# Closing two key or value sums at once on the two halves of TensorE's array

## The chip, the cores and the metric

The kernel runs on one core of a Trainium2 chip, as one program in one launch. The metric is the device time of one execution in microseconds. It is compared as the median of several runs.

## The reference

A decoder of two layers is computed for 8 sequences of 112 tokens with 256 features. Each layer has an attention of its own kind, a cross-attention to a context, and a feed-forward part, each followed by a layer norm. The change lies in the cross-attention of the first layer:

```python
x = _layernorm(x + _L0_xattn_ref(x, ctx_768, Wq, Wk, Wv, Wo, bo), axis=-1)

def _L0_xattn_ref(x, context, Wq, Wk, Wv, Wo, bo):     # x (8,112,256), context (8,375,192)
    h, dh = (16, 64)
    q = (x @ Wq).reshape(B, Nq, h, dh)
    k = (context @ Wk).reshape(B, Nk, h, dh)            # Wk, Wv (192, 1024)
    v = (context @ Wv).reshape(B, Nk, h, dh)
    scores = jnp.einsum('bqhd,bkhd->bhqk', q, k) * dh ** -0.5
    attn = jax.nn.softmax(scores, axis=-1)
    out = jnp.einsum('bhqk,bkhd->bqhd', attn, v).reshape(B, Nq, h * dh)
    return out @ Wo + bo
```

The keys and values of all 8 sequences, `context @ Wk` and `context @ Wv`, are what the change touches. They contract over 192 features, which is one block of 128 and one of 64.

## The kernel before

**The products of keys and values.** TensorE computes them in the format fp32r (F32R in the code), in which one pass of an instruction handles a matmul that takes two passes in fp32. Since one fp32r product is rounded, each operand is split into a rounded high part and the remainder, the low part, and several products are added in one PSUM bank. The main block (128 features) takes three: high x high, high x low, low x high. The second block has 64 features; the host lays these out twice, in rows 0 to 63 and 64 to 127. `ctx_rest` holds the rounded high part of the context in the upper 64 rows and its low part in the lower 64, so that the fourth pass `rest x rest` gives high x high and low x high of that block at once. The fifth pass, `last`, multiplies `ctx_rest` by `w_rest_low`, the low part of the weights, in all 128 rows: high x low and low x low. `exact_products` (L96) lists the five pairs and `accumulate` (L82) issues them; its matmul is at L86. A sixth tensor, `rest_high`, has the rounded high part of the second block in all 128 rows. GpSimd makes it (L670, L794) for its own subtraction, and no matmul reads it.

**Sizes.** A key sum ("k" job) gives 128 of the 1024 key features for 375 context positions (376 columns in the matmul); 8 make the keys of a sequence. A value sum ("v" job) gives 512 value features for 125 positions; 6 make the values.

**Rounds and jobs.** `cross_attention` (from L683) works in rounds -1 to 8. In round i, TensorE computes the heads of sequence i, the queries, keys and values ("front") of sequence i + 1, and the end ("tail") of sequence i - 1. A round has 8 steps u. In each step, TensorE issues in this fixed order: the transposes of the probabilities (`turn`, L845), the scores of the next step (`scores`, L836), the weighing with the values of the step before (`weigh`, L857), and then two or three jobs. The jobs share PSUM banks 0 and 1. The front jobs come in pairs, one on bank 0 and the next on bank 1: u = 0 has q0 and q1, u = 1 to 4 the eight k, u = 5 to 7 the six v. Others come between: in rounds with a tail, job OUT (the output projection) goes ahead of the pair of u = 2 on bank 1, and job NT (transposes at L893) ahead of the pair of u = 5 on bank 1. RB follows the pair of u = 0 on bank 0. In rounds with heads, RA comes at u = 6 on bank 0, behind the pair if there is one: transposes of the softmax divisors at L886. Round -1 has neither heads nor tail, only the front jobs of sequence 0, one behind the other, with the first scores behind step 4.

**Who empties the banks.** Each job's last matmul adds one to `job_ready[b]`. ScalarE then copies bank 0 (L1021, queries L1022), VectorE copies bank 1 (L936, queries L937; OUT is read by L968), and each adds one to `job_used[b]`. A job begins with a wait on `job_used` of its bank for all earlier jobs there. TensorE executes its instructions in order, so a wait at the start of a job holds everything behind it. VectorE's order per step is: copy the turned probabilities (L949), maximum of the next scores (L944), empty bank 1. ScalarE's is: exponentials of the next scores (L1028), empty bank 0.

**Halves of the array.** In `scores`, the two heads of a step have 64 rows each, in rows 0 to 63 and 64 to 127, and write to different banks. In `weigh`, the two heads write to different halves of the output partitions, 64 columns of the array each. The wide cross-attention of the second layer has in its `scores` (L1241, L1244) two matmuls over 128 rows, followed by two over 64 rows each.

Of the kernel before, what the change touches and what calls it, by code (L numbers as in the profile page):

```python
# [19 lines left out]
ST, SP_ = 3, S // 3  # L20
SE = S + 1
CB = DC - 128
# [59 lines left out]
def accumulate(pe, out, pairs):  # L82

    last = None
    for k, (lhs, rhs) in enumerate(pairs):
        last = pe.matmul(out, lhs, rhs, start=(k == 0), stop=(k == len(pairs) - 1))  # L86
    return last
# [8 lines left out]
def exact_products(lhs, rhs):  # L96

    return [(lhs["high"], rhs["high"]), (lhs["high"], rhs["low"]), (lhs["low"], rhs["high"]),  # L100
            (lhs["rest"], rhs["rest"]), (lhs["last"], rhs["last"])]


def wait_past(eng, sem, value):

    if not isinstance(value, int) or value > 0:
        eng.wait_ge(sem, value)
# [22 lines left out]
class Core:  # L130
# [36 lines left out]
    def sem(self, name):  # L167
        self.phase_sems.append(self.nc.alloc_semaphore(name=name))
        return self.phase_sems[-1]
# [513 lines left out]
def cross_attention(core, d, layer):  # L683
# [8 lines left out]
    bank = core.bank  # L692
# [32 lines left out]
    def before(i, b):  # L725

        if isinstance(i, int):
            extra = max(i, 0) + max(i - 1, 0) if b == 0 else 2 * max(i - 1, 0)
            return U * min(i + 1, B) + extra
        return (U + 2) * i + (U - 1 if b == 0 else U - 2)  # L730

    with ExitStack() as ctx:
# [3 lines left out]
        ctx_t, ctx_high, ctx_low, ctx_rest, rest_high = core.ctx_t, core.ctx_high, core.ctx_low, core.ctx_rest, core.rest_high  # L736
        w_high, w_low, w_rest, w_rest_low = core.w_high, core.w_low, core.w_rest, core.w_rest_low
        kt, v, qt = pair("kt", [128, M, S]), pair("v", [SP_, ST, INNER]), pair("qt", [128, M, T])
# [9 lines left out]
        job_ready, job_used = [sem("job_ready0"), sem("job_ready1")], [sem("job_used0"), sem("job_used1")]  # L748
# [27 lines left out]
        with nc.Block() as block:  # L776
            @block.sync
            def _(sp):
                for i in range(2, B):
                    wait_past(sp, split_done, i - 3)  # L780
                    sp.dma_start(ctx_t[i % 2][:, :, :], d["ctx_t"][i].rearrange("(c p) n -> p c n", p=128)).then_inc(ctx_loaded[i % 2], 16)
# [40 lines left out]
            @block.tensor  # L822
            def _(pe):
                ident = core.c(128, C_ID, 128)
                context = lambda q, cols: dict(high=ctx_high[q][:, cols], low=ctx_low[q][:, cols], rest=ctx_rest[q][:, cols],
                                               last=ctx_rest[q][:, cols])
                weights = lambda n, cols: dict(high=w_high[n][:, cols], low=w_low[n][:, cols], rest=w_rest[n][:, cols],
                                               last=w_rest_low[n][:, cols])

                def scores(i, u, p):  # L830
                    if u == 0:
                        pe.wait_ge(job_used[0], before(i - 1, 0) + QK // 2 + (0 if isinstance(i, int) and i <= 1 else 1))
                        pe.wait_ge(job_used[1], before(i - 1, 1) + QK // 2 + (0 if isinstance(i, int) and i <= 1 else 1))
                    for e in range(PER):
                        rows = slice(e * DH, (e + 1) * DH)
                        last = pe.matmul(S_BANK(u, e)[0:T, 0:S], qt[p][rows, u, :], kt[p][rows, u, :], start=True, stop=True)  # L836
                    last.then_inc(s_ready, 1)

                def turn(i, u):
                    for e in range(PER):  # L840
                        pe.wait_ge(p_ready, (i * U + u) * PER + e + 1)
                        if e == 0:
                            wait_past(pe, pt_copied, (i * U + u) * PER)
                        for k in range(ST):
                            last = pe.transpose(T_BANK(u, e)[0:SP_, k * T:(k + 1) * T], PROB(u, e)[:, k * SP_:(k + 1) * SP_], ident[0:T, 0:T])  # L845
                        last.then_inc(pt_ready, 1)

                def weigh(i, u, p):
                    if u == U - 1:
                        pe.wait_ge(pt_copied, (i + 1) * G)  # L850
                    if u % HU == 0:
                        wait_past(pe, ot_ready, 2 * i - 1 + u // HU)
                    at = u % HU * T
                    for k in range(ST):
                        for e in range(PER):
                            g = u * PER + e
                            last = pe.matmul(bank[6 + u // HU][e * DH:(e + 1) * DH, at:at + T], v[p][:, k, g * DH:(g + 1) * DH],  # L857
                                             prob_t[u % 2][e][:, k, :], start=(k == 0), stop=(k == ST - 1))
                    last.then_inc(pv_done, 1)

                def job(i, p, b, n, kind, a):
                    q = 1 - p
                    heads, out = parts(i)[0], bank[b]
                    wait_past(pe, job_used[b], before(i, b) + n)
                    if kind == "q":
                        for m in range(4):
                            last = accumulate(pe, out[:, m * T:(m + 1) * T], [
                                (core.wq[:, c, (4 * a + m) * 128:(4 * a + m + 1) * 128], core.xt[:, c, bass.ts(i + 1, T)])
                                for c in range(KD)])
                    elif kind == "k":  # L870
                        if a == 0:
                            wait_past(pe, split_done, i)
                            if not heads:
                                pe.wait_ge(w_split, 1)
                        last = accumulate(pe, out[:, 0:SE], exact_products(
                            weights("k", slice(a * 128, (a + 1) * 128)), context(q, slice(0, SE))))
                    elif kind == "v":
                        if a == 0 and not heads:
                            pe.wait_ge(w_split, 2)
                        last = accumulate(pe, out[0:SP_, :], exact_products(  # L880
                            context(q, slice(a // 2 * SP_, (a // 2 + 1) * SP_)), weights("v", slice(a % 2 * 512, (a % 2 + 1) * 512))))
                    elif kind in (RA, RB):
                        pe.wait_ge(inv_ready, 2 * i + (1 if kind == RA else 0))
                        for m in range(HU):
                            u = a * HU + m
                            last = pe.transpose(out[:, m * T:(m + 1) * T], inv[:, u * 128:(u + 1) * 128], ident[0:T, 0:T])  # L886
                    elif kind == OUT:
                        pe.wait_ge(ot_ready, 2 * i)
                        last = accumulate(pe, out[0:T, 0:D], [(ot[:, m, :], core.wo[:, m, :]) for m in range(M)])
                    else:  # L890
                        pe.wait_ge(normed_ready, i)
                        for c in range(KD):
                            last = pe.transpose(out[:, c * T:(c + 1) * T], normed[:, c * 128:(c + 1) * 128], ident[0:T, 0:T])  # L893
                    last.then_inc(job_ready[b], 1)

                def round_(i, p):
                    heads, front, tail = parts(i)
                    for u in range(U):
                        if heads:
                            turn(i, u)  # L900
                            if u + 1 < U:
                                scores(i, u + 1, p)
                            elif front:
                                scores(i + 1, 0, 1 - p)
                            if u > 0:
                                weigh(i, u - 1, p)
                        if tail and u == 0:
                            weigh(i - 1, U - 1, 1 - p)
                        for b, n, kind, a in jobs(u, heads, front, tail):
                            job(i, p, b, n, kind, a)  # L910
                        if front and not heads and u == U_KEYS:
                            scores(i + 1, 0, 1 - p)

                rounds(pe, round_)
# [1422 lines left out]
```

## Time and profile before

| | us |
|---|---|
| median of 3 runs | 1117.83 (1116.03 to 1121.14) |
| the profiled execution | 1118.2 |
| its span, first to last instruction | 1116.4 |
| TensorE matmuls busy in the span | 1018.3 (91%) |
| TensorE weight loads busy | 784.8 (70%), beside the matmuls |
| VectorE, ScalarE, GpSimd busy | 579.7, 404.0, 151.0 |
| mean granted TensorE clock | 0.945 of 2.4 GHz |

The span is the time between the first and the last instruction in the trace of one execution; its whole time is 1.8 us more. Matmuls overlap in the trace: a record lasts longer than the step to the next record, so that the sum of durations is no time. The step from one start to the next is what one of a series costs. A matmul in fp32 leaves two records, one for each pass; one in fp32r leaves one. The first cross-attention lies between 126.9 and 476 us.

### The profile page before, as it was taken

How to read it: one execution, taken by the hardware profiler on the slowest of the kernel's cores; microseconds unless marked ns; L12 is line 12 of the kernel's file. 1: busy time of each engine (PE TensorE's matmuls, PEld its weight loads, DVE VectorE, ACT ScalarE, POOL GpSimd, SP SyncE). 2: the span in 40 equal slices, each digit the busy share in tenths (PEclk: the TensorE clock that was granted, in tenths of full speed). 3: DMA queues.
4: the chain of work that ended last, by engine and by line, in shares of the span. 5: the costliest groups of instructions: out<-in, count | busy, mean ns of one | idle time of the engine just before them, and what ended most of it. 6: DMA issues, size and time to landing. Idle time of an engine off the chain costs nothing. (4 is left out here: it accounts for less than half of the span.)

```text
span 1116.4 us, 17912 instructions
## 1 busy us (share of the span) xinstructions
PE 1018.3 (91%) x6672; PEld 784.8 (70%) x6672; DVE 579.7 (52%) x1271; ACT 404.0 (36%) x1029; POOL 151.0 (14%) x151
## 2 busy tenths in 40 slices
PE   6899799999999999779999978787899999999884
PEld 4578677787787776579999964455767777776642
DVE  1786545555555555565556553575244444444315
ACT  2556434333333334254444513466233222322100
POOL 0334311011011000023333412100100000000000
PEclk9999899999999999979999998899899999999955
DMA  4500000000000000092111003300000000010001
GB/s 143 183 2 1 29 14 11 6 14 15 0 0 0 0 0 0 1 312 66 50 38 38 1 1 66 67 2 1 28 1 21 9 14 14 15 27 1 1 0 33
DMA packets 24159, 34.21 MB, mean 31 GB/s; under 512 B 3153, under 2 KB 19762, under 8 KB 24098
## 3 DMA queue, kind: packets, MB, share of 16 engines
q1 hardware_dynamic: 24098, 33.39, 10.0%
q8 instruction: 39, 0.64, 0.2%
q14 instruction: 22, 0.18, 0.1%
HBM read 30.63 MB, written 2.75 MB: 30 GB/s over the span
## 5 line engine op out<-in xcount | busy, mean ns | idle before, releaser
L1028 ACT ACTIVATE x_prob<-bank,x_negmax 112x375 f32<-112x375 f32 x128 | 72.2, 569 | 154.0 <-DVE x_negmax L944 154.0
L1661 DVE TENSOR_TENSOR moe_h_low<-moe_sq,moe_h_high 128x448 fp32r<-128x448 f32 x64 | 54.7, 872 | 52.8 <-ACT moe_h_high L1726 39.6
L1702 POOL TENSOR_TENSOR moe_sq<-moe_r 128x448 f32<-128x448 f32 x64 | 64.0, 1002 | 123.2 <-ACT moe_r L1734 104.7
L86 PE MATMUL bank<-moe_w_low,moe_h_high 128*112 128x256 f32 x256 | 71.8, 280 | 0.0
L86 PE MATMUL bank<-moe_w_high,moe_h_high 128*112 128x256 f32 x256 | 71.7, 280 | 0.0
L86 PE MATMUL bank<-moe_w_high,moe_h_low 128*112 128x256 f32 x256 | 71.7, 280 | 0.0
L944 DVE TENSOR_REDUCE x_negmax<-bank 112x1 f32<-112x375 f32 x128 | 64.1, 542 | 8.0 <-PE bank L836 6.0
L1734 ACT ACTIVATE moe_r<-bank 128x448 f32<-128x448 f32 x64 | 34.9, 545 | 86.9 <-PE bank L86 85.3
L1427 ACT ACTIVATE x_prob<-bank,x_negmax 112x375 f32<-112x375 f32 x64 | 36.1, 568 | 72.6 <-DVE x_negmax L1342 72.6
L949 DVE COPY x_prob_t<-bank 125x336 f32<-125x336 f32 x128 | 58.9, 498 | 6.1 <-PE bank L845 4.2
L857 PEld LDWEIGHTS bank<-x_prob_t,x_v 125*64 125x64 f32 x768 | 37.7, 137 | 34.2 <-issue 30.2
L836 PE MATMUL bank<-x_kt,x_qt 64*112 64x375 f32 x256 | 57.1, 523 | 0.7 <-DVE x_kt L936 0.7
L845 PE MATMUL bank<-const,x_prob 112*125 112x112 f32 x384 | 54.1, 276 | 2.6 <-ACT x_prob L1028 2.4
L845 PEld LDWEIGHTS bank<-const,x_prob 112*125 112x125 f32 x384 | 50.9, 190 | 6.2 <-ACT x_prob L1028 4.8
L86 PE MATMUL bank<-w_in,xt 128*112 128x512 f32 (+2 forms) x128 | 44.6, 490 | 11.3 <-DMA w_in<-in_L_attn_W_in 8.5
L86 PE MATMUL bank<-moe_xt_high,moe_w_high 128*128 128x448 f32 x128 | 48.5, 379 | 3.9 <-DVE moe_w_low L1667 2.7
L857 PE MATMUL bank<-x_prob_t,x_v 125*64 125x112 f32 x768 | 51.4, 270 | 0.0
L1241 PE MATMUL bank<-x_ctx_t,x_qt 128*112 128x375 f32 x128 | 46.8, 488 | 3.5 <-ACT x_prob L1427 2.9
L810 POOL COPY x_inv<-x_inv_head 112x512 f32<-112x512 f32 x16 | 9.8, 614 | 282.3 <-DVE x_inv_head L955 282.3
L1342 DVE TENSOR_REDUCE x_negmax<-bank 112x1 f32<-112x375 f32 x64 | 32.0, 542 | 30.6 <-PE bank L1244 30.6
L86 PE MATMUL bank<-moe_xt_low,moe_w_high 128*128 128x448 f32 x128 | 47.6, 372 | 0.0
L86 PE MATMUL bank<-moe_xt_high,moe_w_low 128*128 128x448 f32 x128 | 47.5, 371 | 0.0
(365 smaller groups left out, 2290.3 us busy)
## 6 DMA issues: line engine op xcount, KB each, us to landing
moe_w<-in_L_ffn_W SPq DMA_DIRECT2D x16, 512.0 KB, 4.7
ctx_t<-in_ctx_t SPq DMA_DIRECT2D x8, 376.0 KB, 4.3
x_ctx_t<-in_ctx_t SPq DMA_DIRECT2D x8, 376.0 KB, 3.1
wk<-in_L_xattn_Wk SPq DMA_DIRECT2D x2, 1024.0 KB, 6.7
wv<-in_L_xattn_Wv SPq DMA_DIRECT2D x2, 1024.0 KB, 9.5
wq<-in_L_xattn_Wq SPq DMA_DIRECT2D x2, 1024.0 KB, 11.5
wo<-in_L_xattn_Wo SPq DMA_DIRECT2D x2, 1024.0 KB, 13.1
w_in<-in_L_attn_W_in SPq DMA_DIRECT2D x1, 1160.0 KB, 7.1
```

The lines of the kernel that those rows point to most:

```text
L86: last = pe.matmul(out, lhs, rhs, start=(k == 0), stop=(k == len(pairs) - 1))
L836: last = pe.matmul(S_BANK(u, e)[0:T, 0:S], qt[p][rows, u, :], kt[p][rows, u, :], start=True, stop=True)
L845: last = pe.transpose(T_BANK(u, e)[0:SP_, k * T:(k + 1) * T], PROB(u, e)[:, k * SP_:(k + 1) * SP_], ident[0:T, 0:T])
L857: last = pe.matmul(bank[6 + u // HU][e * DH:(e + 1) * DH, at:at + T], v[p][:, k, g * DH:(g + 1) * DH], prob_t[u % 2][e][:, k, :], start=(k ...
L944: dve.tensor_reduce(negmax[:, g:g + 1], S_BANK(u, e)[0:T, 0:S], AX_X, ALU.max, negate=True).then_inc(max_ready, 1)
L949: dve.tensor_copy(prob_t[u % 2][e][:, :, :], T_BANK(u, e)[0:SP_, 0:ST * T] .rearrange("s (k t) -> s k t", k=ST)).then_inc(pt_copied, 1)
L1028: act.activation(PROB(u, e)[:, :], S_BANK(u, e)[0:T, 0:S], ACT.Exp, bias=negmax[:, g:g + 1], accum_out=total[:, g:g + 1]).then_inc(p_ready, 1)
L1241: pe.matmul(S_BANK[e][0:T, 0:S], q[:, 2 * j + e, query], c[:, 0, 0:S], start=True, stop=False)
L1427: act.activation(prob[w % 2][e][:, :], S_BANK[e][0:T, 0:S], ACT.Exp, bias=negmax[:, g:g + 1], accum_out=total[:, g:g + 1]).then_inc(e_read ...
L1661: dve.tensor_tensor(h_low[half][:, m, :], sq[m % 2][:, :], h_high[half][:, m, :].bitcast(F32), ALU.subtract).then_inc(low_done, 1)
L1702: pool.tensor_tensor(sq[m % 2][:, :], r[m % 2][:, :], r[m % 2][:, :], ALU.mult).then_inc(sq_done, 1)
L1734: act.activation(r[m % 2][:, :], bank[m][:, 0:HALF], ACT.Relu).then_inc(h_used, 1)
```

## The change

The list of products has four pairs instead of five. A "k" or "v" job on bank 0 now issues its four passes without closing the sum and without announcing it. The job on bank 1 issues its own four, and then `close_sums` issues the fifth pass of both. Each of these is over 64 rows: the sum in bank 0 takes rows 0 to 63 of `w_rest_low` and `rest_high`, the sum in bank 1 takes rows 64 to 127, which hold the same features. It gives high x low of the second block; low x low is not computed any more. Both `job_ready` are announced by these two matmuls.

```diff
-    return [(lhs["high"], rhs["high"]), (lhs["high"], rhs["low"]), (lhs["low"], rhs["high"]),
-            (lhs["rest"], rhs["rest"]), (lhs["last"], rhs["last"])]
+    return [(lhs["high"], rhs["high"]), (lhs["high"], rhs["low"]), (lhs["low"], rhs["high"]), (lhs["rest"], rhs["rest"])]
...
+                def open_sum(out, pairs):
+
+                    for k, (lhs, rhs) in enumerate(pairs):
+                        pe.matmul(out, lhs, rhs, start=(k == 0), stop=False)
+
+                def close_sums(q, kind, a):
+
+                    for b in range(2):
+                        half, at = slice(b * CB, (b + 1) * CB), a + b
+                        if kind == "k":
+                            last = pe.matmul(bank[b][:, 0:SE], w_rest_low["k"][half, at * 128:(at + 1) * 128], rest_high[q][half, :],
+                                             start=False, stop=True)
+                        else:
+                            last = pe.matmul(bank[b][0:SP_, :], rest_high[q][half, at // 2 * SP_:(at // 2 + 1) * SP_],
+                                             w_rest_low["v"][half, at % 2 * 512:(at % 2 + 1) * 512], start=False, stop=True)
+                        last.then_inc(job_ready[b], 1)
...
-                        last = accumulate(pe, out[:, 0:SE], exact_products(
-                            weights("k", slice(a * 128, (a + 1) * 128)), context(q, slice(0, SE))))
+                        open_sum(out[:, 0:SE], exact_products(weights("k", slice(a * 128, (a + 1) * 128)), context(q, slice(0, SE))))
+                        if b == 1:
+                            close_sums(q, "k", a - 1)
+                        return
...
-                        last = accumulate(pe, out[0:SP_, :], exact_products(
+                        open_sum(out[0:SP_, :], exact_products(
                             context(q, slice(a // 2 * SP_, (a // 2 + 1) * SP_)), weights("v", slice(a % 2 * 512, (a % 2 + 1) * 512))))
+                        if b == 1:
+                            close_sums(q, "v", a - 1)
+                        return
```

## Rows read from the trace of the kernel before

**Rows 1.** Windows: length, busy us and count of each engine, clock, DMA share.

```profile
192.00:233.00 41.00, 40.96 (x304) 32.06 (x304) 22.87 (x52) 15.03 (x44) 4.29 (x8) 1.00 0.04 11
...
126.90:476.00 349.10, 337.37 (x2432) 262.88 (x2432) 193.40 (x420) 122.42 (x354) 34.39 (x47) 0.98 0.03 7
```

**Rows 2.** Waits, 126.9 to 476 us: waited for, us in total, times, longest.

```profile
PEld bank L86 <- DVE xt L936: 2.8, 6, 0.5
...
PE bank L86 <- DVE x_qt L937: 1.6, 1, 1.6
```

**Rows 3.** Timeline, end of the stage: start, us, what.

```profile
475.24 0.37 SPq L1537 DMA_DIRECT2D moe_wg<-in_L_ffn_Wg  x1
```

**Rows 4.** Groups by line and form, 126.9 to 476 us, TensorE.

```profile
L86 PE MATMUL bank<-ctx_rest,wk_rest_low 128*128 128x376 f32 x64 | 21.5, 335 | 0.0
...
L86 PE MATMUL bank<-wv_rest_low,ctx_rest 128*125 128x512 f32 x48 | 18.8, 392 | 0.0
```

**Rows 5.** Timeline, the end of two key sums and the next step.

```profile
249.99 0.33 PE L86 MATMUL bank<-ctx_high,wk_low 128*128 128x376 f32 x1
...
251.19 0.80 PEld L845 LDWEIGHTS bank<-const,x_prob 112*125 112x125 f32 x6
251.37 0.81 PE L845 MATMUL bank<-const,x_prob 112*125 112x112 f32 x6
...
252.10 0.89 PE L836 MATMUL bank<-x_kt,x_qt 64*112 64x375 f32 x4
...
252.92 0.80 PE L857 MATMUL bank<-x_prob_t,x_v 125*64 125x112 f32 x12
...
253.65 0.44 PE L86 MATMUL bank<-ctx_high,wk_high 128*128 128x376 f32 x1
...
253.92 0.33 PE L86 MATMUL bank<-ctx_low,wk_high 128*128 128x376 f32 x1
```

**Rows 6.** Timeline, TensorE in the wide cross-attention (from several narrow windows).

```profile
1032.92 0.48 PE L1241 MATMUL bank<-x_ctx_t,x_qt 128*112 128x375 f32 x1
1033.23 0.48 PE L1241 MATMUL bank<-x_ctx_t,x_qt 128*112 128x375 f32 x1
1033.64 0.89 PE L1244 MATMUL bank<-x_ctx_t,x_qt 64*112 64x375 f32 x4
1034.05 0.48 PE L1244 MATMUL bank<-x_ctx_t,x_qt 64*112 64x375 f32 x2
1034.46 0.91 PE L1253 MATMUL bank<-const,x_prob 112*125 112x112 f32 x6
1038.94 0.82 PE L1253 MATMUL bank<-const,x_prob 112*125 112x112 f32 x6
```

**Rows 7.** Timeline, v2's fifth pass to job RA.

```profile
263.97 0.39 PE L86 MATMUL bank<-wv_rest_low,ctx_rest 128*125 128x512 f32 x1
...
264.40 0.59 ACT L1021 COPY x_v<-bank 125x512 f32<-125x512 f32 x1 [0.28 <-PE bank L86]
...
265.36 0.55 PE L886 MATMUL bank<-const,x_inv 112*128 112x112 f32 x4
```

**Rows 8.** Timeline, bank 1 behind OUT and behind NT.

```profile
245.81 0.42 DVE L968 TENSOR_TENSOR x_res<-bank,x 112x256 f32<-112x256 f32 x1 [3.54 <-PE bank L86]
...
246.28 0.44 PE L86 MATMUL bank<-ctx_high,wk_high 128*128 128x376 f32 x1
...
258.96 0.40 PE L86 MATMUL bank<-wv_rest_low,ctx_rest 128*125 128x512 f32 x1
258.98 0.34 DVE L936 COPY xt<-bank 128x224 f32 x1
...
259.37 0.50 PE L86 MATMUL bank<-wv_high,ctx_high 128*125 128x512 f32 x1
```

**Rows 9.** Timeline, k2's fifth pass in the first round and ScalarE's copy.

```profile
138.18 0.34 PE L86 MATMUL bank<-ctx_rest,wk_rest_low 128*128 128x376 f32 x1
...
138.55 0.47 ACT L1021 COPY x_kt<-bank 128x375 f32<-128x375 f32 x1 [3.14 <-PE bank L86]
```

More of the change, by code:

```diff
@@ L824, in _ @@
                 ident = core.c(128, C_ID, 128)
[L825 to L828, printed above, removed]
+                context = lambda q, cols: dict(high=ctx_high[q][:, cols], low=ctx_low[q][:, cols], rest=ctx_rest[q][:, cols])
+                weights = lambda n, cols: dict(high=w_high[n][:, cols], low=w_low[n][:, cols], rest=w_rest[n][:, cols])
+                def open_sum(out, pairs):
[11 more added lines that the diff above has]
+                        last.then_inc(job_ready[b], 1)
                 def scores(i, u, p):
```

## Prediction

> **What bounds the kernel now.** I read the windows of the first cross-attention first [rows 1]: between 126.9 and 476 us TensorE is busy for 337.4 of 349.1 us, and in a middle stretch (192 to 233 us, one batch) for 40.96 of 41.00 us at a granted clock of 1.00, the 2.4 GHz level, while VectorE and ScalarE are busy for 22.9 and 15.0 us. So in this stage every nanosecond of TensorE's own sequence is a nanosecond of the kernel. The waits [rows 2] say the same from the other side. Few waits stand before TensorE's instructions; two matter here. Six times a weight load of L86 waited for VectorE's copy at L936, 0.46 us each, and once a matmul waited 1.6 us for L937. After the stage nothing absorbs a shift: the next stage's first DMA is issued at 475.24 us [rows 3], behind the barrier that ends this one, so what this stage gains or loses the kernel gains or loses.
>
> The groups of matmuls [rows 4] give the counts: 64 fifth passes for keys (128 rows, 376 columns) and 48 for values (512 columns), so 32 and 24 pairs. Their mean durations, 335 and 392 ns, are no prices, since matmuls overlap; the price is the step from one start to the next. In the timeline of two key sums [rows 5] eight steps go from 249.99 to 251.37, 0.172 us each; in value sums [rows 7] six steps go from 263.97 to 265.36, 0.232 us each. At most the change can halve this: 32 x 0.172 + 24 x 0.232 = 11.1 us.
>
> **What the pair itself costs.** The change takes two full passes out and puts in a pair on 64 rows each. The trace before has no such pair in this number format, but has the same figure in two places, and there the reader is to see what surrounds it.
>
> First, are the two halves simultaneous? In [rows 5] the scores at L836 are four records (two matmuls, two passes each) of 375 columns. One pass of that width at full height steps by 0.31 us (1032.92 to 1033.23, [rows 6]); the four records take 252.10 to 252.92, 0.82 us, and one after the other they would need 1.25. So the halves do run at once.
>
> Second, what does going in and out cost? The transposes before the scores take 0.73 us (251.37 to 252.10) for six, of which the five steps inside are about 0.11 each; the last is 0.20. The wide cross-attention [rows 6] has just the sequence of the changed kernel: full-height matmuls at L1241, the half-height pair at L1244, full-height transposes at L1253.
> - Last full pass to pair: 1033.23 to 1033.64, 0.41 against 0.31. So some 0.09 us for emptying the array before its division changes.
> - First pass of the pair to its second: 1033.64 to 1034.05, again 0.41. So 0.10 for a weight load that no matmul covers.
> - Second pass to the transposes: 1034.05 to 1034.46, 0.41. So 0.09 for emptying again. (The three steps together are 1.23 us, where three of 0.31 are 0.93 to 0.94; with the rows' rounding I split the excess as 0.09, 0.10 and 0.09.)
> - The six transposes then take 0.91 us; the same six not behind a pair take 0.82. So 0.09 to 0.10 for the first load behind the pair. In [rows 5] a key sum behind the column-divided matmuls of L857 shows it too: 253.65 to 253.92 is 0.27 where 0.17 is the step. Today the loads for the transposes begin at 251.19, under the last fifth pass.
>
> The Trainium skill (TensorEngine Tiling (Array Packing), Tiling Modes, Key Properties) says that changing the tiling mode drains the engine; the trace agrees, 0.09 us each way. The same page (Overview, Theoretical Speedup) promises up to twice the rate for 64 rows or fewer; that promise is without the drain, and is the rival "free switches" below.
>
> With 0.01 for the start of the second half, a pair costs 0.09 + 0.10 + 0.01 + 0.172 + 0.09 + 0.10 = 0.56 us for keys, where two passes cost 0.344: +0.22. For values 0.62 against 0.464: +0.16. The pass of the pair in this format is unseen: its bounds are one full pass (both at once, as the scores) and two (no overlap). I take one, since the scores are the nearest row. The loads are bounded by nothing (hidden, as between full passes) and 0.10 each; I take 0.10, the row with the same neighbours.
>
> **The moved semaphore.** Bank 0's sum was complete, and announced, a whole sum ahead of bank 1's. Now both are announced behind the pair. Where something wants bank 0 immediately behind the pair, TensorE waits for ScalarE, and all that is queued behind it (the next transposes, scores and jobs) waits too.
>
> Ordinary pairs are followed by transposes and scores in other banks, more than 2 us, so ScalarE's 0.47 to 0.59 us copy is hidden: 28 key pairs (rounds 0 to 6, four each; in three of the other four the stall takes over) and 15 value pairs (two in each of seven rounds, one in the first). 28 x 0.22 + 15 x 0.16 = 6.2 + 2.4 = 8.6 us.
>
> Job RA: at u = 6 of seven rounds bank 0 gets v2, bank 1 v3, and then bank 0 gets the transposes of L886. Today [rows 7] v2's fifth pass starts at 263.97, ScalarE copies at 264.40 (0.43 later) for 0.59 us and is done at 264.99, before v3's last pass ends and RA starts at 265.36. Counted from where the first fifth pass would have started, RA can now start after 0.09 + 0.11 + 0.43 + 0.59 + 0.05 (semaphore; 259.32 to 259.37 in [rows 8]) = 1.27 us, and pays 0.10 for its load: 1.37 against 0.464, +0.90. Seven times, 6.3 us.
>
> NT: v1 waits today for VectorE to empty bank 1 of NT (copy 258.98 to 259.32, v1 at 259.37, [rows 8]); that instant does not move, but v0's fifth pass, which filled 0.232 us of the wait, now comes behind v1. Six times: +1.4 us. OUT: k3 starts at 246.28, 0.05 after VectorE's read of bank 1 ends (245.81 + 0.42, [rows 8]); k2's fifth pass no longer fills the time. Six times 0.172: +1.0 us.
>
> The first round, without heads, runs jobs back to back. k2's fifth pass starts at 138.18 and ScalarE's copy at 138.55 takes 0.47 [rows 9]. Behind (k2,k3) and (k4,k5): 0.09 + 0.11 + 0.37 + 0.47 + 0.05 for the wait and 0.05 more of load than now, 1.14 against 0.344, +0.80 each. Behind (k0,k1) +0.97, as k0's fifth pass lies in the 1.6 us wait of [rows 2] and taking it away brings nothing. Behind (v0,v1) and (v2,v3) +0.90 each as for RA. Behind (k6,k7) the scores wait for k7's copy anyway: about 0. Together 4.4 us.
>
> Nothing else is added: no DMA, no queue is passed, and GpSimd already makes the half that is now read. The one place in which the change saves work unseen by these sums would be an idle TensorE, and there is none.
>
> Sum: 8.6 + 6.3 + 1.4 + 1.0 + 4.4 = 21.7 us. The profiled execution took 1118.2 us (span 1116.4), 0.4 above the median of the three runs shown. 1118.2 + 21.7 = 1139.9; against the median 1139.5. I say **1139.7 us**, slower by 1.9%.
>
> **Rivals.**
> - *Loads hidden.* The loads of pair and successor go under running matmuls. For it: full passes do so. Against: at L1244, L1253 and L836 they don't. It takes 0.10 off all 56 pairs and another 0.10 off some 50 successors: 10.6 us, 1129.
> - *Halves one after the other.* For it: no pair of this format is in the trace. Against: the scores. Adds 32 x 0.172 + 24 x 0.232 = 11.1: 1151.
> - *Free switches* (the skill's promise alone). Pairs -0.16 and -0.22: 28 and 15 of them -7.8; RA 1.08 against 0.464, seven times, +4.3; NT and OUT +2.4; first round, by the same subtraction, +3.1. Sum +2.0: 1120, within 0.5%. Against: all of [rows 6].
> - *Faster.* The halved passes outweigh all, because a pair delays nothing but itself: bank 0's copy is never waited for. That gives 11.1 - 2.4 (NT, OUT) = 8.7 us, 1109.5. The point from which it decides is the price of going in and out, 0.38 us a pair by the rows: under 8.7 / 56 = 0.15 it would win if no copy were waited for. Against: even at a price of nothing the waits leave +2 (above), for at RA ScalarE needs 1.02 us from the pass's start.
>
> **How the numbers follow.** Main case 0.70 (its own range 1134 to 1145, from 0.05 us a pair and 0.2 a stall either way), loads hidden 0.12, one after the other 0.10, free switches 0.05, faster 0.03. The bounds of pass and load are 1129 and 1151; the range that holds all but 0.1 to 0.15 is 1128 to 1151. 0.5% (5.6 us) is about what a measurement of this kernel tells from no change. Slower 0.92, same 0.05, faster 0.03.
>
> **What the changed profile would show.** The timeline: a pair of 64-row records 0.01 apart, 0.27 (keys) or 0.33 us (values) after the start of the last full pass; the next transposes some 0.37 or 0.43 us after the pair, their six taking 0.9. In the waits: TensorE's L886 waiting seven times for ScalarE's L1021, some 0.7 us each; the wait of L86 for L936 six times at 0.7 instead of 0.46; in the first round new waits of L86 for L1021. The stage ends near 498 instead of 476 us, a middle round takes some 2.5 us more, and the windows behind it are the same but shifted. I would be wrong if the pair started 0.17 behind the last pass, if its two halves were 0.17 apart, or if RA did not wait.

## The result, and the profile after

The changed kernel takes 1137.88 us (median of 6 runs, 1134.83 to 1143.09), the kernel before 1116.2 us (6 runs, the three shown ahead of the prediction among them, 1113.71 to 1121.14). The ratio is 1.0196 with an interval of 1.0164 to 1.0228: slower by 22 us (18 to 25). The prediction said 1139.7 us, slower.

Where the time went can be read in the first cross-attention alone. These rows of the changed kernel's timeline mark the two ends of the stage and a middle round: the first query matmul of the stage, that of rounds 2 and 3, and the first matmul of the next stage.

```profile
125.71 0.53 PE L86 MATMUL bank<-xt,wq 128*128 128x112 f32 x1 [1.45 <-PEq L174]
...
239.01 0.36 PE L86 MATMUL bank<-xt,wq 128*128 x1
...
282.70 0.36 PE L86 MATMUL bank<-xt,wq 128*128 x1
...
498.45 0.36 PE L86 MATMUL bank<-moe_wg,xt 128*112 128x8 f32 x1 [4.66 <-DMA moe_wg<-in_L_ffn_Wg]
```

The kernel before has these at 126.93, 231.42, 272.74 and 479.02. The stage grew from 352.1 to 372.7 us, +20.65; the middle round from 41.32 to 43.69. (Over rounds 1 to 5, the middle rounds of which both ends can be seen in this way, the means are 41.28 and 43.63, which are the numbers used below.) The span grew by 19.2 us, as the stage began 1.2 us earlier in this execution; everything behind it is only shifted. The mark that the prediction looked at, the first DMA of the next stage, moved for the same reason from 475.24 to 494.56 us, not to 498. The rounds by themselves, from the same starts:

| | before | changed | more | the sum said |
|---|---|---|---|---|
| first round (-1) | 26.30 | 30.78 | 4.48 | 4.5 |
| round 0 | 36.92 | 38.91 | 1.99 | 2.1 |
| rounds 1 to 5, mean | 41.28 | 43.63 | 2.35 | 2.5 |

Round 6 is like them. It and the end of the stage together took 2.4 us more.

An ordinary key pair of the changed kernel, timeline (start, length, what), to lay beside [rows 5]:

```profile
254.71 0.34 PE L830 MATMUL bank<-ctx_rest,wk_rest 128*128 128x376 f32 x1
...
254.97 0.19 PEld L837 LDWEIGHTS bank<-rest_high,wk_rest_low 64*128 64x128 f32 x2 [0.24 <-issue]
254.98 0.44 PE L837 MATMUL bank<-rest_high,wk_rest_low 64*128 64x376 f32 x2
255.34 0.73 PEld L859 LDWEIGHTS bank<-const,x_prob 112*125 112x125 f32 x6 [0.18 <-issue]
255.35 0.91 PE L859 MATMUL bank<-const,x_prob 112*125 112x112 f32 x6
```

The two 64-row matmuls are one row of x2, 0.44 us long in all: they run at once. But the pair starts 0.27 us behind the last full pass instead of 0.17, its load starts with it (and did not lie under the pass before), the transposes start 0.37 us behind it, again with their load, and take 0.91 us instead of 0.81. From 254.71 to 255.35 and with that 0.10 more, less the full pass's own 0.172, the pair costs 0.57 us, where two fifth passes cost 0.344: +0.22, as summed. The same rows of the values give 0.62 (268.65 to 269.40, and 0.10 more, less 0.232), against 0.464: +0.16.

```profile
268.65 0.40 PE L830 MATMUL bank<-wv_rest,ctx_rest 128*125 128x512 f32 x1
268.98 0.49 PE L840 MATMUL bank<-wv_rest_low,rest_high 64*125 64x512 f32 x2
269.40 0.36 PE L859 MATMUL bank<-const,x_prob 112*125 112x112 f32 x1
```

The place at RA, timeline of the changed kernel, to lay beside [rows 7]:

```profile
273.51 0.39 PE L830 MATMUL bank<-wv_rest,ctx_rest 128*125 128x512 f32 x1
273.83 0.50 PE L840 MATMUL bank<-wv_rest_low,rest_high 64*125 64x512 f32 x2
...
274.36 0.59 ACT L1040 COPY x_v<-bank 125x512 f32<-125x512 f32 x1 [1.38 <-PE bank L840]
...
275.07 0.60 PE L905 MATMUL bank<-const,x_inv 112*128 112x112 f32 x4 [0.75 <-ACT x_v L1040]
```

From v2's first pass to RA's first matmul it is 3.30 us instead of 2.43, and RA's four matmuls take 0.05 more: +0.92, seven times. At OUT, k3 starts 1.08 us behind OUT's last matmul in both kernels: k2's fifth pass, 0.172, had filled time that is now empty. The waits (waited for, us in total, times, longest), of TensorE in the stage:

```profile
PE bank L905 <- ACT x_v L1040: 5.2, 7, 0.7
...
PE bank L830 <- ACT x_kt L1040: 1.7, 3, 0.6
...
PE bank L830 <- ACT x_v L1040: 1.3, 2, 0.7
```

None of these three stands in the waits of TensorE's matmuls before. They are RA, and the five places of the first round where a pair is followed by its own bank. With 28 and 15 ordinary pairs (6.2 + 2.3), RA (6.4), OUT (1.0), the first round (4.3) and NT (0.4, below) the rows add up to 20.6 us, which is the stage.

### The profile page after: what moved, and what is told of

The parts are those of the page before. It is cut to its first block and busy times, and to the rows that moved or that the text cites. A ratio compares the mean times of both kernels' runs of the same rounds, so it can differ in the third digit from the quotient of the medians.

```text
span 1135.6 us, 17912 instructions
## 1 busy us (share of the span) xinstructions
PE 1028.0 (91%) x6672; PEld 770.6 (68%) x6672; DVE 582.0 (51%) x1271; ACT 406.5 (36%) x1029; POOL 150.6 (13%) x151
## 5 line engine op out<-in xcount | busy, mean ns | idle before, releaser
L963 DVE TENSOR_REDUCE x_negmax<-bank 112x1 f32<-112x375 f32 x128 | 64.2, 543 | 12.4 <-PE bank L850 11.2
L859 PE MATMUL bank<-const,x_prob 112*125 112x112 f32 x384 | 58.3, 287 | 2.6 <-ACT x_prob L1047 2.4
L859 PEld LDWEIGHTS bank<-const,x_prob 112*125 112x125 f32 x384 | 47.7, 189 | 13.6 <-issue 8.8
```

The costliest lines, as they stand in the source:

```text
L963: dve.tensor_reduce(negmax[:, g:g + 1], S_BANK(u, e)[0:T, 0:S], AX_X, ALU.max, negate=True).then_inc(max_ready, 1)
```

## The experiments

Where a comparison is by rounds, it is the step from one round's first query matmul to the next one's, mean of rounds 1 to 5, in the profile of that run. This is steadier than the medians.

**The announcement alone.** The closing passes are made over all 128 rows, with the operands of the kernel before:

```diff
-                        half, at = slice(b * CB, (b + 1) * CB), a + b
+                        half, at = slice(0, 128), a + b
...
-                            last = pe.matmul(bank[b][:, 0:SE], w_rest_low["k"][half, at * 128:(at + 1) * 128], rest_high[q][half, :],
+                            last = pe.matmul(bank[b][:, 0:SE], w_rest_low["k"][half, at * 128:(at + 1) * 128], ctx_rest[q][half, :],
...
-                            last = pe.matmul(bank[b][0:SP_, :], rest_high[q][half, at // 2 * SP_:(at // 2 + 1) * SP_],
+                            last = pe.matmul(bank[b][0:SP_, :], ctx_rest[q][half, at // 2 * SP_:(at // 2 + 1) * SP_],
```

> The changed kernel with one thing undone: the two closing passes run over all 128 rows with the operands of the kernel before, one after the other, still behind both sums and still announcing both banks. So the array is never divided for them, and the moved announcement stays. My theory (division and waits are separate prices): against the kernel before, RA waits 7 x (0.43 + 0.59 + 0.05 + 0.05 - 0.464) = 4.6 us, the first round 3.3, OUT 1.0, NT 6 x 0.232 = 1.4, in sum +10.3 us, 1126.5; against the changed kernel -11.4. Rival 'it is all the division': equal to before, 1116. Rival 'it is all the waits': equal to the changed kernel, 1138.

Measured: 1130.94 us against 1117.16, ratio 1.0108 (1.0078 to 1.0138). A middle round takes 42.43 us: +1.15 over before, where the sum of RA (0.66), OUT (0.17) and NT (0.23) said 1.06; with the 0.05 that RA's first load costs too, 1.11. So neither rival holds: of the 2.35 us of a middle round, about half (1.15) is the moved announcement and half (1.20) the division. TensorE's waits show RA with the shorter wait that the missing division leaves:

```profile
PE bank L905 <- ACT x_v L1040: 3.6, 7, 0.5
```

By the medians the kernel is 13.8 us slower than before, where 10.3 had been expected (the interval is 8.7 to 15.4). Of the difference 2.2 us lie in the first round, which took 31.8 us instead of 29.6, at a granted clock of 0.50 in the window from 137 to 142 us (the clock comes below).

**Both passes in the same half.**

```diff
-                        half, at = slice(b * CB, (b + 1) * CB), a + b
+                        half, at = slice(0, CB), a + b
```

> The changed kernel with both closing passes in rows 0 to 63, so that they can't overlap. If the two halves really work at once, each pair gets one pass longer where TensorE's own sequence sets the pace: 28 x 0.172 + 15 x 0.233 + 0.17 = +8.5 us against the changed kernel, about 1146; behind RA and in the first round nothing is added, since bank 0's pass still comes first. Rival 'the halves ran one after the other anyway': equal to the changed kernel.

Measured: 1150.32 us, ratio to before 1.0295 (1.026 to 1.033). A middle round takes 44.73 us, 1.10 more than in the changed kernel, where 4 x 0.172 + 2 x 0.233 said 1.15. The timeline of a key pair:

```profile
260.22 0.34 PE L830 MATMUL bank<-ctx_rest,wk_rest 128*128 128x376 f32 x1
260.49 0.61 PE L837 MATMUL bank<-rest_high,wk_rest_low 64*128 64x376 f32 x2
261.02 0.36 PE L859 MATMUL bank<-const,x_prob 112*125 112x112 f32 x1
```

The pair is followed after 0.53 us instead of 0.37. Over all pairs outside the first round that the transposes follow, the second pass adds 0.166 us for keys and 0.235 for values (medians), a full pass each. So the halves do work at once in the changed kernel, and that is worth the whole second pass. The median is further away from the changed kernel's (12.4 us) than the 8.5 expected; rounds 0 to 6 account for 7.8, and the first round, 33.6 us, ran partly at the low clock.

**Each sum closed alone.**

```diff
-                    for b in range(2):
-                        half, at = slice(b * CB, (b + 1) * CB), a + b
+                    if True:
+                        half, at = slice(b * CB, (b + 1) * CB), a
...
-                        if b == 1:
-                            close_sums(q, "k", a - 1)
+                        close_sum(q, "k", a, b)
...
```

> Each job closes its own sum with a 64-row pass alone, directly behind its four passes: bank 0 is announced as early as before, but the array is divided 112 times instead of 56 and no two halves run at once. By the steps in the changed kernel's trace each costs 0.09 + 0.19 + 0.10 = 0.38 to 0.39 us more than a full pass, 112 of them 43 us, of which some 2.5 lie in waits that are there anyway (NT, OUT, k1): +41 us against before, 1157. Rival 'loads and emptying are hidden when one sum is closed at a time': at most +10, 1126.

Measured: 1157.54 us against 1117.16, ratio 1.0339 (1.0297 to 1.0381), and 46.25 us a middle round: +4.97. The 14 closings of a round at 0.38 to 0.39 are 5.4, less about 0.3 at v1 and 0.1 at k3, which wait anyway. (The profiled execution, 1165.4 us, is the slowest of the four; its first round took 39.1 us, with a clock of 0.50 in the windows from 137 to 152 us.) The timeline of one closing, between two sums:

```profile
260.52 0.34 PE L830 MATMUL bank<-ctx_rest,wk_rest 128*128 128x376 f32 x1
260.78 0.43 PE L837 MATMUL bank<-rest_high,wk_rest_low 64*128 64x376 f32 x1
261.15 0.44 PE L830 MATMUL bank<-ctx_high,wk_high 128*128 128x376 f32 x1
261.42 0.33 PE L830 MATMUL bank<-ctx_low,wk_high 128*128 128x376 f32 x1
```

Steps of 0.26, 0.37 and 0.27 stand where three of 0.17 stood. This is the price of one visit to the divided array, without any wait; the change pays it once for two sums.

**RA's pair as before.** The value sums v2 and v3 are made in full passes:

```diff
+                        if a in (2, 3):
+                            cols, feats = slice(a // 2 * SP_, (a // 2 + 1) * SP_), slice(a % 2 * 512, (a % 2 + 1) * 512)
+                            last = accumulate(pe, out[0:SP_, :], exact_products(context(q, cols), weights("v", feats)) + [
+                                (ctx_rest[q][:, cols], w_rest_low["v"][:, feats])])
+                            last.then_inc(job_ready[b], 1)
+                            return
```

> The changed kernel, but the value sums v2 and v3, the pair ahead of RA, are made as before the change (five full passes, each announced by itself); the other 48 pairs are closed in halves. If RA's wait costs what I worked out, 7 x 0.92 us go, and 0.9 more in the first round behind the same pair: -7.3 us against the changed kernel, 1130.6. Rival 'the wait at RA is covered by later work, only the division counts': -8 x 0.15 = -1.2 us.

Measured: 1135.47 us against 1117.16, ratio 1.0140 (1.0105 to 1.0175). By the ratios this is 6 us less than the changed kernel, by the medians 2.4; neither is sharp. A middle round is 42.72 us, 0.91 less, where 0.92 was worked out for RA and 0.15 for the rival. The wait at RA is gone from the list, and v2's first pass to RA's is 2.43 us again. The first round did not follow: 36.25 us in this profile, instead of 29.9.

**The clock of the first round.** The same kernels again, for their profiles:

> The kernel ra_plain once more, for its profile alone. Its first profile had 36.25 us in the first round, at clock 0.50 from 137 to 153 us, and 42.7 in the middle rounds. If the slow stretch is a property of the execution and not of the kernel, the first round is 29.9 us with the clock at 1.00, and the middle rounds 42.7 again.

> The changed kernel once more, for its profile alone: the middle rounds at 43.6 us again. Whether the first round is 30.8 again is open: if its waits can let the clock fall, as they did in the profiles of full_height, same_half, alone and ra_plain, it may be 31 to 37 with a stretch at clock 0.50; if the kernel's first profile is typical, 30.8.

Measured: ra_plain 1133.22 us, middle rounds 42.72, first round 33.9; the changed kernel 1143.34 us, middle rounds 43.62, first round 37.0 instead of 30.8. The windows of this second profile of the changed kernel (length, busy us of TensorE, loads, VectorE, ScalarE, GpSimd, granted clock, DMA share and GB/s) show why:

```profile
132.00:137.00 5.00, 2.10 (x10) 1.47 (x10) 3.77 (x4) 0.00 (x0) 0.00 (x0) 0.98 0.00 0
137.00:142.00 5.00, 3.88 (x13) 2.77 (x11) 1.10 (x2) 0.94 (x2) 0.00 (x0) 0.50 0.00 0
142.00:147.00 5.00, 4.44 (x13) 3.62 (x14) 0.55 (x1) 0.47 (x1) 0.00 (x0) 0.50 0.00 0
147.00:152.00 5.00, 4.23 (x13) 2.37 (x13) 0.72 (x2) 0.47 (x1) 0.00 (x0) 0.50 0.00 0
152.00:157.00 5.00, 4.33 (x15) 2.96 (x16) 1.53 (x3) 1.80 (x5) 0.00 (x0) 0.81 0.00 0
```

and those of the first:

```profile
132.00:137.00 5.00, 2.38 (x12) 1.49 (x10) 3.53 (x5) 0.35 (x1) 0.00 (x0) 1.00 0.00 0
137.00:142.00 5.00, 4.02 (x20) 3.02 (x20) 0.96 (x3) 0.81 (x3) 0.00 (x0) 1.00 0.00 0
```

Behind the same wait of TensorE (1.8 us for VectorE's copy of q1 in both) the granted clock fell to 1.2 GHz (0.50) in one execution and stayed at 2.4 GHz (1.00) in the other. It stayed low until about 154 us and cost 6.2 us. Not all was equal ahead of the fall: all kernels begin the stage at 1.2 GHz, and in the second profile the clock rose earlier (0.67 in the window from 126 to 132 us, against 0.57), so that the queries were done earlier and TensorE waited 1.3 us instead of 0.4 for `wk_rest_low`. By itself this costs nothing, since the first key sum starts 6.9 us behind the stage's start in both. Nor does it decide alone: in same_half that wait was 0.3 us and the clock fell, in beside_scores 1.4 and it stayed. The expectation that a second profile of ra_plain would be at full clock was wrong. The Trainium skill (TensorE: Matmul & The Clock Gate, Part 1) says that the window in which the chip watches TensorE's activity is free-running and doesn't reset when a kernel starts, so that the same kernel warms up differently from run to run. The two profiles agree with it in that one kernel had two different clocks (0.50 and 1.00 from 137 to 142 us), but here in the middle of the kernel; that the free-running window is the reason no run here shows.

**The first round as before.** The seven pairs of round -1 are made in full passes (the edit of ra_plain, under `if not heads`, for both kinds of sum).

> The changed kernel, but the seven pairs of the first round, which has no heads between them, are made as before the change. My theory: the first round gives back 4.5 us (30.8 us from the first query matmul to the next round's instead of 26.3), the later rounds stay at 43.6 us: 1133.4. Rival 'the waits of the first round also let the clock fall in some executions, and that costs more than the waits': more than 4.5 us in the median, and no stretch at clock 0.50 between 137 and 155 us in the profile.

Measured: 1132.7 us against 1115.98, ratio 1.0143 (1.0116 to 1.017); the first round is 26.30 us, to the hundredth that of before, with a clock of 1.00 in every window from 132 us on, and the middle rounds 43.63. In the medians 5.2 us are given back, by the ratios 5.9. The 4.5 us of theory fit within the noise, and a part of the clock's price may be in the rest; the medians can't separate the two.

**Four passes.** The kernel before without the fifth pass.

```diff
-            (lhs["rest"], rhs["rest"]), (lhs["last"], rhs["last"])]
+            (lhs["rest"], rhs["rest"])]
```

> The kernel before without any fifth pass (the output lacks the products of the second block's context with the low part of its weights). It measures what the fifth passes are worth where they stand: 64 x 0.172 + 48 x 0.232 = 22.1 us, less what they fill today (OUT 1.0, NT 1.4, k0 and the copies of the first round 0.3): -19.4 us, 1096.8. Rival 'the step from start to start overstates a pass, something else is close behind': clearly less than 15 us.

Measured: 1099.35 us against 1116.9, ratio 0.9846 (0.9828 to 0.9863), so 15 to 19 us less, where 19.4 had been expected. The stage lost 18.4 us, but 2.1 of them are a shorter wait for the next stage's weights at its end (2.5 us instead of 4.6). The first round gave 0.4 of the 2.5 us expected of it: the clock fell there too (0.71 in the window from 137 to 142 us, where before had 1.00). A middle round takes 38.95 us, 2.33 less, where 8 x 0.172 + 6 x 0.232 less 0.17 (OUT) and 0.23 (NT) said 2.36. The step from start to start is a pass's price, and the fill at OUT and NT is real.

**Closed beside the scores.** The pairs of u = 1, 3, 4 and 7 stay open and are closed between the transposes and the scores of the next step; the others are made in full passes. In the first round only the pair of u = 7 is left open.

```diff
+        def beside(u, heads, front):
+            return front and u in ((1, 3, 4, 7) if heads else (7,))
...
                             turn(i, u)
+                            open_ = left(i, p, u, heads, front, tail)
+                            if open_:
+                                close_sums(open_[0][4], open_[0][2], open_[0][3])
                             if u + 1 < U:
                                 scores(i, u + 1, p)
...
                             copy_turned(i, u)
+                            empty_left(dve, i, p, u, 1, heads, front, tail, copy)
                             if u + 1 < U:
                                 row_max(i, u + 1)
```

`left` lists the sums that the step before left open, and `empty_left` empties them, in ScalarE ahead of the exponentials.

> The idea of the change, put where the array is divided anyway and nothing waits. In rounds with heads the pairs (k0,k1), (k4,k5), (k6,k7) and in all rounds (v4,v5) stay open and are closed in halves one step later, between the transposes and the scores, which are 64 rows high too; ScalarE and VectorE empty them ahead of the next exponentials and the next row maxima. All other pairs are made as before the change. A pair then costs one pass and no own going in and out: 21 x (0.344 - 0.18) + 8 x (0.464 - 0.24) = 3.4 + 1.8 = 5.2 us less than before, 1111. Rival 'the array empties between the fp32r pair and the fp32 scores too': +0.19 a pair, about the same as before, 1116. Rival 'VectorE's copy ahead of the row maxima makes the next transposes wait': each such step loses 0.2 to 0.5 us, slower than before by up to 5 us.

Measured: 1110.84 us (12 runs) against 1116.9 (17 runs), ratio 0.9950 (0.9934 to 0.9967): faster than both kernels, by 4 to 7 us against before. The timeline of a key pair:

```profile
236.97 0.81 PE L872 MATMUL bank<-const,x_prob 112*125 112x112 f32 x6
...
237.70 0.44 PE L850 MATMUL bank<-rest_high,wk_rest_low 64*128 64x376 f32 x2
...
237.98 0.79 PE L863 MATMUL bank<-x_kt,x_qt 64*112 64x375 f32 x4
238.18 0.47 ACT L1068 COPY x_kt<-bank 128x375 f32<-128x375 f32 x1 [1.50 <-PE bank L850]
238.32 0.54 DVE L982 COPY x_kt<-bank 128x375 f32<-128x375 f32 x1
...
238.71 0.80 PE L884 MATMUL bank<-x_prob_t,x_v 125*64 125x112 f32 x12
```

From the transposes to the pair it is 0.73 us, as it is to the scores in [rows 5], and from the pair to the weighing 1.01 instead of 0.82: the pair costs 0.19 us, since the emptying and the uncovered load are paid there anyway. Both rivals fall: the array does not empty there, and the round is shorter, not longer. A middle round takes 40.28 us, 1.00 less than before, where 3 x 0.164 + 0.224 is 0.72. The remainder is at NT: VectorE is earlier there, from NT's first matmul to v1 it is 1.43 us instead of 1.61, and as v1 no longer waits, its load is covered.

**The pair of u = 5 as well.**

> The kernel with pairs closed beside the scores, with the pair (v0,v1) of u = 5 closed so too. In the run beside_scores VectorE emptied NT's bank at 255.93 us, 0.26 before v0's fourth pass ended, so v1 need not wait. Each of seven rounds saves another 0.464 - 0.24 = 0.22 us: a middle round falls from 40.28 to about 40.06, the whole by 1.5 us. Rival 'v1 waits for VectorE again, as the fifth pass of v0 is missing as filling': middle rounds unchanged at 40.28.

```diff
-            return front and u in ((1, 3, 4, 7) if heads else (7,))
+            return front and u in ((1, 3, 4, 5, 7) if heads else (7,))
```

Measured: 1109.2 us (6 runs) against 1115.98 (10 runs), ratio 0.9939 (0.9918 to 0.9959). A middle round takes 40.06 us, 0.22 less again, as expected; the two medians alone would not tell these two kernels apart. The stage takes 342.9 us against 352.1, 9.2 less; rounds 0 to 6 account for 8.3 of them. The rest lies in its last rounds, where before had a granted clock of 0.81 from 453 to 462 us and this kernel 1.00 from 453 to 465.

## Why the prediction was right

**The bound.** TensorE's own order set the stage: what each edit added to it, the stage grew by, in a middle round to 0.05 us or so once NT is set right, in all experiments but one (beside_scores, 0.1 off until v1's covered load is counted).

**The pair's price.** 0.56 and 0.62 us were worked out from the fp32 pair of the wide cross-attention [rows 6]; 0.57 and 0.62 were measured. The upper bound of the range was a real alternative: the experiment in one half shows what it would have looked like. The lower, loads that are hidden, no run built. The rivals "loads hidden" and "free switches" fall with the `issue` rows of the loads above and with the run alone.

**The moved announcement.** RA 0.92 (0.90 worked out), OUT 0.17 (0.17), the first round 4.5 (4.5 with its last value pair). The stalls are in no row of before; they came out of two of its times, the pass-to-copy time of 0.43 and the copy's 0.59 us, laid behind the new order.

**The mis-sized term** is NT, 1.4 us in the sum, 0.4 measured. The step that failed is "that instant does not move". The timeline of the kernel before, beside [rows 8], and then that of the changed kernel:

```profile
257.75 0.41 PE L893 MATMUL bank<-const,x_normed 112*128 112x112 f32 x2
```

```profile
266.38 0.41 PE L912 MATMUL bank<-const,x_normed 112*128 112x112 f32 x2
...
267.45 0.34 DVE L955 COPY xt<-bank 128x224 f32 x1
...
267.84 0.50 PE L830 MATMUL bank<-wv_high,ctx_high 128*125 128x512 f32 x1
```

From NT's first matmul to v1 the changed kernel takes 1.46 us, the kernel before (257.75 to 259.37) 1.62. VectorE's copy came 0.16 us earlier behind TensorE's work, so that the lost filling of 0.232 cost only 0.07. That the division does it and not the announcement is shown by full_height, where the interval is 1.61 as before and the whole 0.23 is lost. (For the same reason v1's weight load waited 0.53 us, 3.2 in six times, and not the 0.7 forecast.) How: ahead of NT, VectorE works through a chain (copy of k7, normalising, copying, turned probabilities) that starts with the end of k7, while TensorE now spends 0.1 us more on the transposes behind it. Counted from the first of these transposes (means of rounds 1 to 5), VectorE begins to copy k7 at 0.14 us instead of 0.20, because the last pass of k7 ends earlier against them, and NT begins at 2.38 instead of 2.28; from the copy of k7 to that of NT's bank VectorE takes 3.30 us in both. The two shifts, 0.06 and 0.10, are the 0.16. In same_half, whose pair is longer, the copy of k7 begins at 0.11 and the interval is 1.42 instead of 1.45: the 0.03 appear there too.

**The clock** was left out. The sum holds for executions in which the first round keeps 2.4 GHz from 132 us on. In the second profile the first round cost 10.7 us more than before, not 4.5. No row of before showed whether waits of 0.6 us, repeated, would matter to it. Seven profiles are of kernels whose first round closes its sums in the way of the change or of one of its parts (the changed kernel and ra_plain twice each, full_height, same_half, alone); in six of them the window from 137 to 142 us has a clock of 0.50 to 0.57. In the four with a first round as before (before, first_plain, beside_scores, beside_five) it has 1.00, and in four_passes, which announces each sum by itself but has one pass less in it, 0.71. That the thinner work of TensorE in this round lets the clock fall is likely, and not shown: these are few executions.

**The base.** The sum was made on the profiled execution of 1118.2 us; with three later runs the median of the kernel before is 1116.2. So 1139.7 was 1.8 too high while the difference, 21.7 us, was met: in the profile the stage grew by 20.65 us, 1.1 less than the sum, mostly at NT, and the clock in some runs may have gone the other way. That the medians differ by just the 21.7 us of the sum is luck; their ratio allows 18 to 25.

## What to carry to other kernels

Halving a pass as short as these by dividing the array pays only if the array is divided there anyway: look in the timeline for the neighbour that already has that height and put the pair beside it; by itself, each visit costs the emptying twice and two uncovered loads, here 0.38 us, more than a 0.17 or 0.23 us pass. Before two sums are closed together, ask what waits for the first of them: the semaphore that moves back is a cost of its own, here as large as the division. And where two jobs fill another engine's latency, work taken out of the filler is worth nothing.

## What was not expected of the hardware

The 64-row pair in fp32r is over in 0.44 us for both halves, where one of them lasts 0.437, so that the second starts 0.003 us or so behind the first (0.01 had been put in), and a 64-row pass takes as long as a full one: in one half, the second pass adds 0.166 us for keys and 0.235 for values. The other is the clock: in the same kernel, some 17 us of the first round were granted 1.2 GHz in one execution and 2.4 in another, 6.2 us apart.
